# An eight-layer graph and expert network: expert weights spread two per up product until they are two behind, and sixteen reductions on VectorE spread over two gathers

## The reference

```python
def experts(x, gate_w, w1, w2):            # layers 0, 1 and 3; 8 experts, width 192 or 128
    h = layernorm(x)
    c = top2_weights(h @ gate_w.T)         # one weight per node and expert, zero for six of the eight
    y = 0
    for e in range(8):
        y += (act(h @ w1[e]) * c[:, e:e + 1]) @ w2[e]
    return x + y

def gcn(x, W1, W2, adj):                   # layer 1, twice a gather and a product
    h = relu(norm(adj) @ x @ W1)
    return x + norm(adj) @ h @ W2

# attention scores of layer 2's second convolution: a = (x @ W2.T) . att  =  x @ (W2.T . att)
```

## Time and profile before

| what | value |
|---|---|
| median of 3 runs | 1759.04 us (1754.56 to 1760.23) |
| profiled execution, its own time | 1759.04 us |
| its span | 1757.3 us |
| TensorE busy | 1692.5 us, 96% |
| VectorE, ScalarE, GpSimd busy | 53%, 26%, 39% |
| mean granted clock of TensorE | 0.983 |

### The profile page before, as it was taken

One profiled execution on the slowest core, in us unless ns is written; L12 is line 12 of the kernel. 1 busy time (PEld: TensorE's weight loads), 2 busy tenths in 40 slices (PEclk: granted clock), 3 DMA queues, 4 the chain that ended last, 5 costly groups with the idle time before them and its releaser, 6 DMA issues.

```text
span 1757.3 us, 25860 instructions
## 1 busy us (share of the span) xinstructions
PE 1692.5 (96%) x10227; PEld 1587.7 (90%) x10227; DVE 933.1 (53%) x1879; ACT 463.1 (26%) x875; POOL 693.0 (39%) x428
## 2 busy tenths in 40 slices
PE   8799999999999988899899999999999999999999
PEld 7699999997999988899377788989999999998999
DVE  8993446417865679957497554423112141235731
ACT  6444123203222138924223211101011011112320
POOL 1026855552445531051020075532644434342654
PEclk9899999999999999899899999999999999999999
DMA  2002221323111210014010021111211111110212
GB/s 89 1 28 73 74 72 63 136 74 126 63 55 60 68 55 10 1 46 140 8 43 1 1 90 60 61 48 37 73 63 54 47 53 59 50 54 29 73 63 71
DMA packets 41999, 99.83 MB, mean 57 GB/s; under 512 B 10508, under 2 KB 12142, under 8 KB 41894
## 3 DMA queue, kind: packets, MB, share of 16 engines
q1 hardware_dynamic: 37828, 87.87, 15.7%
q10 hardware_dynamic: 4066, 10.46, 1.7%
HBM read 96.39 MB, written 1.92 MB: 56 GB/s over the span
## 4 chain that ended last, share of the span: by engine, by line
PE 81%; DVE 11%; ACT 4%; POOL 2%; issue 1%; POOLq 0%; DVEq 0%; ACTq 0%
PE bank L2396 10%; PE bank L2398 10%; PE bank L2397 10%; PE banks L2396 9%; PE banks L2397 9%; PE banks L2398 9%; PE bank L2959 3%; PE banks L2959 3%; PE bank L3036 3%; PE bank L3041 3%; PE banks L3036 2%; PE banks L3041 2%; DVE src_hot L1469 1%; DVE tmp L1803 1%; PE banks L2811 1%
## 5 line engine op out<-in xcount | busy, mean ns | idle before, releaser
L823 POOL TENSOR_TENSOR w_hi<-raw,ones_r 128x768 fp32r<-128x768 f32 (+1 forms) x192 | 294.5, 1534 | 1009.6 <-PE banks L2398 369.5
L826 POOL TENSOR_TENSOR w_lo<-raw,w_hi 128x768 fp32r<-128x768 f32 (+1 forms) x192 | 372.8, 1941 | 15.1
L2396 PE MATMUL bank<-w_hi,xT_hi 128*125 128x384 f32 (+2 forms) x560 | 188.6, 337 | 2.3 <-DVE small L1943 1.2
L2398 PE MATMUL bank<-w_hi,xT_lo 128*125 128x384 f32 (+2 forms) x560 | 187.3, 334 | 0.0
L2397 PE MATMUL bank<-w_lo,xT_hi 128*125 128x384 f32 (+2 forms) x560 | 187.2, 334 | 0.0
L2396 PE MATMUL banks<-w_hi,xT_hi 128*125 128x384 f32 (+2 forms) x440 | 151.7, 345 | 0.0
L2397 PE MATMUL banks<-w_lo,xT_hi 128*125 128x384 f32 (+2 forms) x440 | 151.4, 344 | 0.0
L2398 PE MATMUL banks<-w_hi,xT_lo 128*125 128x384 f32 (+2 forms) x440 | 151.3, 344 | 0.0
L1594 DVE TENSOR_TENSOR hT_lo<-tmp,hT_hi 128x312 fp32r<-128x312 f32 (+1 forms) x88 | 92.1, 1051 | 42.4 <-ACT hT_hi L966 42.0
L2396 PEld LDWEIGHTS bank<-w_hi,xT_hi 128*125 128x125 f32 x560 | 104.6, 187 | 5.9 <-POOL w_lo L826 1.5
L2397 PEld LDWEIGHTS bank<-w_lo,xT_hi 128*125 128x125 f32 x560 | 104.6, 187 | 2.5
(11 more groups left out here) (579 smaller groups left out, 3937.7 us busy)
## 6 DMA issues: line engine op xcount, KB each, us to landing
raw<-wa SPq DMA_DIRECT2D x92, 384.0 KB, 3.0
raw<-wc SPq DMA_DIRECT2D x76, 384.0 KB, 3.0
raw<-wb SPq DMA_DIRECT2D x28, 448.0 KB, 3.3
w_rows<-w_in ACTq DMA_DIRECT2D x1, 3072.0 KB, 12.8
bias<-bias_in ACTq DMA_DIRECT2D x6, 384.0 KB
w_first<-w_in ACTq DMA_DIRECT2D x1, 2304.0 KB, 9.1
w_down<-w_down_in SPq DMA_DIRECT2D x8, 288.0 KB, 5.3
w_up<-w_up_in SPq DMA_DIRECT2D x1, 2304.0 KB, 10.8
```

The source lines that it names most:

```text
L823: pool.tensor_tensor(w_hi[:, k, 0:width], raw[:, k, 0:width], ones[:, 0:1].to_broadcast([P, width]), ALU.mult).then_inc(S("unit_high"), 1)
L826: pool.tensor_tensor(w_lo[:, k, 0:width], raw[:, k, 0:width], f(w_hi[:, k, 0:width]), ALU.subtract).then_inc(S("unit_split"), 1)
L2396: tell_used(pe.matmul(dst, l_hi, r_hi, start=start, stop=False))
L2398: return pe.matmul(dst, l_lo, r_hi, start=False, stop=stop)
```

## The change

It has three parts.

1. `spread_after` is a new list of which spreads stand behind which up product. None stands behind the first six; from up product 6 on two follow each product until the spreads are two jobs behind, then one follows each. Behind the last up product stand its own step's spread and two more. `plan_groups` and TensorE's queue both use it, so the banks are handed out anew.
2. ScalarE's rounded copies follow the same list: the copy of job i stands behind the activation with which its spread is issued, or in front of it where the slot of `tmp` is needed.
3. The sixteen reductions: five now stand between the low parts of the first gather, two behind them, two between the sixth and the seventh tile, six between the low parts of the second gather, and one behind the work on `adj` that follows.

```diff
+def spread_after(jobs):
+
+    steps, done = [], 0
+    for j in range(jobs):
+        until = min(done + 2, j - 1) if j >= EXPERT_LAG else 0
+        steps.append(range(done, until))
+        done = until
+    return steps + [range(done, jobs)]
...
-        for j in range(jobs + lag):
+        for j, spread in enumerate(spread_after(jobs)):
...
-            if j >= lag:
-                add(f + "_cB", j - lag, f + "_weighted", j - lag + 1)
+            for i in spread:
+                add(f + "_cB", i, f + "_weighted", i + 1)
...
-                for j in range(jobs + TSLOTS - 1):
+                weighted = full == s + "_weighted"
+                steps = spread_after(jobs) if weighted else [range(max(j - TSLOTS + 1, 0), max(j - TSLOTS + 2, 0))
+                                                             for j in range(jobs + TSLOTS - 1)]
...
+                made = 0
+                for j, spread in enumerate(steps):
                     if j < jobs:
                         m, c = job_of(s, j)
                         cn = CH[c][1]
+                        if made <= j - TSLOTS:
+                            high(made)
+                            made += 1
                         await_group(act, s + "_hidden", j)
...
+                    for i in spread:
+                        if i == made:
+                            high(i)
+                            made += 1
...
-            def messages_low(key, label, k, first=0):
+            def messages_low(key, label, k, first=0, beside=None):
...
                        ).then_inc(S(key + "_low"), 1)
+                    if beside:
+                        beside(i)
...
-            messages_low("g1a", "g1a_agg", KD)
+            def fold_second(first, last):
...
+            messages_low("g1a", "g1a_agg", KD, beside=lambda i: fold_second(i // 2 - 1, i // 2) if i % 2 and i > 1 else None)
...
-            fold_second(0)
+            fold_second(5, 7)
...
                 if i == NT:
-                    fold_second(1)
-            messages_low("g1b", "g1b_agg", KD)
+                    fold_second(7, 9)
+            messages_low("g1b", "g1b_agg", KD, beside=lambda i: fold_second(9 + i // 2, 10 + i // 2) if i % 2 else None)
...
+            fold_second(15, 2 * HEADS)
...
-                for j in range(jobs + EXPERT_LAG):
+                for j, spread in enumerate(spread_after(jobs)):
...
-                    if j >= EXPERT_LAG:
-
+                    if j == EXPERT_LAG:
                         pe.wait_ge(*E(s + "_combineT", NT))
-                        i = j - EXPERT_LAG
+                    for i in spread:
                         m, (c0, cn) = i // 2, CH[i % 2]
```

More of the change, by code:

```diff
@@ L951, in hidden, with high @@
                 jobs = 2 * tiles
-                for j in range(jobs + TSLOTS - 1):
+                weighted = full == s + "_weighted"
+                steps = spread_after(jobs) if weighted else [range(max(j - TSLOTS + 1, 0), max(j - TSLOTS + 2, 0))
+                                                             for j in range(jobs + TSLOTS - 1)]
+                def high(i):
+                    m, c = job_of(s, i)
+                    c0, cn = CH[c]
+                    act.wait_ge(*E(full, i + 1))
+                    act.activation(hT_hi[:, m, c0:c0 + cn], tmp[:, i % TSLOTS, 0:cn], ACT.Copy
+                                   ).then_inc(S(s + "_high"), 1)
+                made = 0
+                for j, spread in enumerate(steps):
                     if j < jobs:
@@ L1846, in _ @@
             add_bias("g1")
-            messages_low("g1a", "g1a_agg", KD)
+            def fold_second(first, last):
+                dve.wait_ge(*E("w2_loaded", 32))
+                for made in range(first, last):
+                    kind, k = divmod(made, HEADS)
+                    if made >= 2:
+                        dve.wait_ge(*E("second_folded", made - 1))
+                    dve.tensor_tensor_reduce(fold_junk[:, made % 2], w2_rows[:, k], att_2[:, kind], 1.0, 0.0, ALU.mult,
+                                             ALU.add, a_part[:, 2 * k + kind:2 * k + kind + 1]
+                                             ).then_inc(S("second_folded"), 1)
+            messages_low("g1a", "g1a_agg", KD, beside=lambda i: fold_second(i // 2 - 1, i // 2) if i % 2 and i > 1 else None)
             dve.wait_ge(*E("g2_fold_high", 1))
```

## The result

The changed kernel takes 1742.47 us (median of 4 runs, 1738.16 to 1743.69), the kernel before 1759.28 us beside it (4 runs, 1754.56 to 1760.23). The ratio is 0.9903, 95% interval 0.9888 to 0.9918. The forecast was 1743.5. A second set of runs of the same kernel gave 1743.22 against 1759.56 (ratio 0.9909, 0.9894 to 0.9924). The profiled execution of after lasted 1741.73 us with a span of 1740.0, 17.3 us shorter than the span of before.

What follows compares the result with a forecast made beforehand. TensorE, busy 96% of the span, was taken as the bound, so only its standstills and lower clock could pay. 7.4 + 5.1 + 3.4 - 0.4 = 15.5 us gave 1743.5 from 1759.0; range 1739 to 1747.5, with rival A 1738.5 to 1751.5.

Steps and rivals of the forecast that it cites:

- The gaps: Ends of three expert layers: last up matmul to down product shortens, gaining 2.51, 2.33 and 2.52, together 7.4 us.
- The loop that I read in the earlier trace: Expert layers' ends: job 22's activation needs job 16's `tmp` slot, whose low part follows weighing 17; spread 17 is issued late.
- its copy and low part follow inside the next step: Steady part of expert layers: job j-2 is weighed behind step j; copy and low part fit the next 2.8 us step.
- The clock: Behind the three layer ends: without the lower-clock stays, 1.70, 1.71 and 1.70 are saved, together 5.1 us; bounds 0 and 5.1.
- No drop of the clock without the gap: Behind the three layer ends: once the order leaves no gap, the clock isn't expected to drop; 5.1 us taken.
- A drop behind every gap: Behind the three layer-end gaps, granted clock 0.63, 0.69 and 0.63 over 4.6, 5.5 and 4.6 us, counted as 5.1 us.
- rival A: Clock drops although gaps are gone, 1748.6; or gather keeps its stall and the load costs 1.5, 1748.0; chance 0.20.
- The folding: Reductions moved: second gather's 3.4 us stall goes (bounds 1.5 and 3.4); first gather loses 0.4 to a load (0 to 1.5).
- B: Nothing arrives: each wait passes to the next bank, or the order doesn't do what it says; 1759 us, chance 0.08.
- C: Slower: in the catching up every low part waits out a GpSimd split, costing 32 us, 1775 us; chance 0.04.
- over 1.05 us throughout: Catching up in expert layers: the slower case starts once a low part costs this, and outweighs the gain at 1.7.
- The 15.5: Whole kernel: summed gain in us, 7.4 + 5.1 + 3.4 - 0.4, taking 1759.0 to 1743.5.

Runs made afterwards that it cites:

- experiment 3: Changed kernel with spreads five behind the up product in place of two, copies where the kernel before has them; 1746.76 us, ratio 0.9926 to the kernel before.
- experiment 4: Changed kernel with ScalarE's expert-layer copies back in the old order, five activations behind, spreads left two behind; 1745.65 us, ratio 0.9925 to the kernel before.
- Experiment 5: Changed kernel with TensorE waiting for the last weighing before each down product: 1753.45 us; with 12 filler matmuls a layer ahead of that wait: 1749.92 us.
- the folding alone: Kernel before with only the sixteen reductions placed as in the changed kernel; 1755.42 us, ratio 0.9983 to the kernel before.
- the wait: Changed kernel with TensorE not opening an expert layer's down product before VectorE has weighed the last job, no filler matmuls; 1753.45 us.

## Why the prediction was right

**The gaps (7.4).** Measured by the same starts: 3.67 - 0.57 - 0.58 = 2.52, then 3.49 - 0.56 - 0.58 = 2.35 and 3.68 - 0.59 - 0.58 = 2.51. The term holds to 0.02 us a layer. The loop that I read in the earlier trace rows is the right one, but experiment 3 corrects what breaks it: not that three spreads in place of seven stand behind the last product, but that the spreads come at least one job earlier, with the copies left where they were. The further step from five to two is worth 1.8 us, and only with the copies in step: by experiment 4 the spreads at two without them lose 2.8. My "its copy and low part follow inside the next step" silently used that part of the change, which I had not priced.

**The clock (5.1).** From the start of the down product on the lead grew by another 1.56, 1.61 and 1.58 us, 4.75 together, where I had 1.70 each: length times missing share is a little too much. Experiment 5 shows the cause apart from the idle time. "No drop of the clock without the gap" held in every trace with closed gaps. "A drop behind every gap" did not: in the four traces with a gap at the end of each layer (before twice, the folding alone, the wait) 11 of 12 have a drop, and the second trace of before has two of three. So for the median over runs 5.1 is an upper bound, and my own range should have had that case in it beside rival A.

**The folding (3.4 and -0.4).** 3.48 and -0.46; alone 3.5 and 0 in the trace, 2.8 in the medians. The steps held: tile 6 is read at 454.00, as forecast (457.3 less the lead of 3.2 us), and the last tile at 460.57, far ahead of the 469.6 that I had as the latest time. Few operations waited out a split (the lowering L1905 took 2.19 us in place of 0.55 once in the rows above). The rule of the Trainium skill (SBUF — State Buffer, "Who interferes with whom"), by which this node work should be blocked by the splits, agrees with that row, and with the reductions. In before five of the sixteen took 2.2 to 2.6 us, three of them among the eight in front of tile 6, so these waits were some 4 us of what made the tile late; in after all sixteen take 939 to 959 ns. One of those, at 431.01, still meets a split that starts at 431.09, and there it is the split that takes longer, 2.19 us. The rule's warning against the change had no price, because only a few operations stand beside a split. The three of before:

```profile
459.83 2.22 DVE L1861 CUSTOM_DVE_ANT_0 fold_junk<-w_rows,att 128x768 f32<-128x768 f32 x1
...
461.98 2.59 DVE L1861 CUSTOM_DVE_ANT_0 fold_junk<-w_rows,att 128x768 f32<-128x768 f32 x1
...
464.51 2.21 DVE L1861 CUSTOM_DVE_ANT_0 fold_junk<-w_rows,att 128x768 f32<-128x768 f32 x1
```

**The rivals.** A fell: the drops are gone and so is the gather's stall. B fell, and its ground was a misreading: the list of waits splits one cause into entries by bank and line, and the five that name ScalarE's `tmp` in before (2.2, 1.2, 1.0, 1.0 and 0.9) add up to 6.3 us. C fell: TensorE waits for nothing between 280 and 330, though the mean low part rose from 1051 ns to 1078. My condition, "over 1.05 us throughout", was met by the mean of all 88, but it is the catching up's low parts that count: the first eight of each layer have means of 0.88, 1.02 and 0.90 us, with single ones up to 1.74.

**What came beside it.** The 15.5 met 15.2 at the places that it named. The span shrank by 17.3 because the attention stage came in its short form in one trace and in its long form in the other. The medians, 16.8 and 16.3 apart, are 1.1 to 1.6 more than the places explain. That the forms of the untouched stages fall unevenly on the two kernels is the likely reason; it isn't shown.

## What to carry to other kernels

Follow a chain of small waits through every queue that it passes, and ask at which distance it closes: here one job less of distance freed a loop over three engines, and going from five jobs to two brought 1.8 us more, if a second engine's order went along. A product that is moved in the queue isn't saved: measure from before its old place to behind its new one. Where TensorE stands still for about 2 us, look at the granted clock behind it and book both, but book the drop as likely, not as certain; here filling the stretch with matmuls did as much for the clock as closing it, and nothing for the idle time. Before a gain of a few us is credited to an edit, compare the stages that it doesn't touch: here one of them moved by 2.6 us with the same instructions in the same order.

## What the runs showed of the hardware

An idle time of TensorE of 1.9 us (starts 2.1 us later) brought the granted clock to 0.63 over the next 4.6 us, and one of 0.2 us behind twelve small matmuls didn't. Two traces of one kernel differed at the same gap of 3.7 us: once a drop that cost 1.5 us, once none. The same instructions in the same order took 139.9 or 142.6 us, at a mean clock of 0.95 or 0.93. A wait that holds TensorE also moved GpSimd's next split, so that VectorE's work got faster: the wait was 0.8 us shorter than the trace without it said. And a meeting of VectorE and GpSimd was paid by either side: a reduction of 0.95 us took up to 2.59 beside a split in before, and a split took 2.19 us beside a reduction of 0.95 in after, where others took 1.47.
